# Turning y of later groups on VectorE instead of TensorE: a fused two-layer residual kernel in fp32r halves

## The reference, cut to what matters

```python
x = x + (einsum('bsd,bdh->bsh', x, L0_W[cat]) + L0_b[cat][:, None, :])        # y
h = gelu(einsum('bnd,hd->bnh', x, fc1_w) + fc1_b)                            # exact gelu
shared = einsum('bnh,sh->bns', h, fc2_w) + fc2_b                              # 384 columns
expert = einsum('bnh,bph->bnp', h, experts_w[idx]) + experts_b[idx][:, None, :]   # 128 columns
out = x + concatenate([shared, expert], -1)
```

## Time and profile before

| | |
|---|---|
| three runs, median | 1683.79 us |
| the profiled execution, own time | 1683.98 us |
| its span | 1682.1 us |
| mean granted clock of TensorE | 0.995 |
| TensorE busy | 1663.5 us (99%) |
| VectorE, ScalarE, Pool busy | 1146.4, 555.2, 200.4 us |
| read from and written to memory | 194.20 and 16.78 MB |

### The profile page before, as it was taken

The page is one execution under the profiler, slowest core; times in us unless marked ns, Lnnn a source line. Parts: engine busy times, 40 slices in busy tenths (PEclk is TensorE's granted clock), DMA queues, the critical chain, the costliest instruction groups (busy, mean ns, idle before and its releaser), DMA issues.

```text
span 1682.1 us, 27867 instructions
## 1 busy us (share of the span) xinstructions
PE 1663.5 (99%) x7305; PEld 1344.5 (80%) x7305; DVE 1146.4 (68%) x1944; ACT 555.2 (33%) x927; POOL 200.4 (12%) x195
## 2 busy tenths in 40 slices
PE   7899999999999999999999999999999999999999
PEld 4688888888888888888888888888888888888887
DVE  4677767677676766857767676776767667676654
ACT  4343233233333333333333333333333333332321
POOL 0010200101010110200202011110200102001010
PEclk8999999999999999999999999999999999999999
DMA  7875546555565565655555465555655546565430
GB/s 208 182 177 129 124 110 150 118 134 119 115 155 106 140 128 104 143 120 136 120 125 130 108 158 110 134 125 110 151 115 132 128 100 146 117 141 119 97 51 25
DMA packets 749465, 211.95 MB, mean 126 GB/s; under 512 B 676008, under 2 KB 690488, under 8 KB 749372
## 3 DMA queue, kind: packets, MB, share of 16 engines
q1 hardware_dynamic: 740732, 203.75, 55.2%
q10 hardware_dynamic: 8640, 7.34, 1.5%
HBM read 194.20 MB, written 16.78 MB: 125 GB/s over the span
## 4 chain that ended last, share of the span: by engine, by line
PE 97%; SPq 1%; DMA 1%; issue 0%; DVE 0%; ACT 0%; DVEq 0%
PE ps_out L732 43%; PE ps_e L717 21%; PE ps_h L717 21%; PE ps_y L704 10%; PE ps_t L654 1%; PE ps_e L654 1%; SPq L333 1%; SPq L313 0%; DMA prep_raw<-in_L_cond_fc_w 0%; SPq L286 0%; DMA w_raw<-in_L_cond_W 0%; DMA exps<-in_itok_B 0%; DVE resid L590 0%; PE ps_h L704 0%; PE ps_h L702 0%
## 5 line engine op out<-in xcount | busy, mean ns | idle before, releaser
L732 PE MATMUL ps_out<-w2e,h 128*128 128x512 f32 x3072 | 761.8, 396 | 0.0
L732 PEld LDWEIGHTS ps_out<-w2e,h 128*128 128x128 f32 x3072 | 573.6, 188 | 135.0
L717 PE MATMUL ps_h<-y_t,w 128*128 128x512 f32 x1536 | 376.9, 395 | 0.0
L717 PE MATMUL ps_e<-y_t,w 128*128 128x512 f32 x1536 | 375.5, 394 | 1.4 <-DVE y_t L520 1.4
L717 PEld LDWEIGHTS ps_e<-y_t,w 128*128 128x128 f32 x1536 | 290.0, 189 | 65.8 <-DVE y_t L520 1.8
L717 PEld LDWEIGHTS ps_h<-y_t,w 128*128 128x128 f32 x1536 | 288.7, 188 | 66.7
L442 ACT CAST w_split<-w_raw 128x512 fp32r<-128x512 f32 x256 | 157.8, 617 | 301.4 <-PE ps_y L704 284.3
L520 DVE TENSOR_TENSOR w_split<-w_raw,w_split 128x512 fp32r<-128x512 f32 x256 | 185.8, 726 | 95.2 <-ACT w_split L442 94.9
L578 DVE CAST h<-g_raw 128x512 fp32r<-128x512 f32 x256 | 116.4, 455 | 191.5 <-ACT g_raw L471 190.9
L409 POOL TENSOR_TENSOR x_raw<-x_raw,b_all 128x512 f32<-128x512 f32 x60 | 79.0, 1317 | 1338.5 <-DMA x_raw<-in_x 1338.5
L457 ACT CAST w2e<-e_whole 128x512 fp32r<-128x512 f32 x256 | 158.7, 620 | 190.8 <-PE ps_out L732 190.8
(11 more groups left out here) (56 smaller groups left out, 422.9 us busy)
## 6 DMA issues: line engine op xcount, KB each, us to landing
w_raw<-in_L_cond_W SPq DMA_DIRECT2D x256, 256.0 KB, 2.9
e_blocks<-in_L_cond_experts_w SPq DMA_DIRECT2D x1024, 64.0 KB, 2.5
out<-resid SPq DMA_DIRECT2D x64, 256.0 KB, 3.3
x_blocks<-in_x SPq DMA_DIRECT2D x240, 64.0 KB, 2.4
b_all<-in_L_cond_b SPq DMA_DIRECT2D x60, 256.0 KB, 3.4
x_raw<-in_x SPq DMA_DIRECT2D x60, 256.0 KB, 3.1
prep_raw<-in_L_cond_fc_w ACTq DMA_DIRECT2D x27, 256.0 KB, 3.9
be_all<-in_L_cond_experts_b SPq DMA_DIRECT2D x64, 64.0 KB, 3.0
```

Of the source, the lines that this page charges most:

```text
L717: last = nc.tensor.matmul(h_bank(c)[:, :], w1[:, w, k, c * P:(c + 1) * P], y_t[:, a, k, :, :].rearrange("p b s -> p (b s)"), start=(k == 0 ...
L732: last = nc.tensor.matmul(ps_out[b][:, :], h[:, c % 2, a, b * S:(b + 1) * S], fc2_columns(c, c % 2, w, b), start=(c == 0 and n == 0), stop ...
```

## The change

- The four turns of y of every later group leave TensorE. ScalarE's queue stores each y to an internal DRAM tensor y_rows (store_y, the step after y_sum) and, at the end of that step, loads it back as exchanged blocks into x_blocks (load_y_blocks, four transfers); VectorE transposes it two steps after y_sum (turn_y). The four turned batches are kept in two tiles of w_raw (y_hold), in x_whole_t and in ps_t until y_high and y_low at the end of the body, which now wait for the group's last fc1 themselves.
- L0's slices go in pairs in the steps of L0_STEPS, so that the last is done in step 12 and not 15.
- W of later groups has two places (WSLOTS = 2); in the first group eight, four of them in the half of e_blocks that is free then (W0SLOTS). b0_rows moves to y.
- SP's order: experts one step earlier (c % 4 of 0 and 1), store(g - 1) at step 2 after the loads of steps 0 and 1, load_x_blocks of batches 0 to 3 at steps 0, 1, 6 and 10; in the start, the experts begin at j = 8, two transfers a slice; the first loads of group 1 and the biases come in step 0 of body(0).
- Pool's add_out_bias waits for y_ready instead of y_turned.

```diff
-    WSLOTS = 4
+    WSLOTS = 2
+    W0SLOTS = 8
+    L0_STEPS = (1, 3, 5, 7, 9, 10, 11, 12)
...
-        w_raw = sb("w_raw", [P, WSLOTS, D])
+        w_raw = sb("w_raw", [P, WSLOTS + 2, D])
...
+        y_hold = w_raw[:, WSLOTS:WSLOTS + 2, :]
+        y_rows = nc.dram_tensor("y_rows", (GB, P, D), F32, kind="Internal").ap()
...
+            return four((y_hold[:, 0, :], y_hold[:, 1, :], x_whole_t[:, :], ps_t)[b])
...
+        def slices_in(c):
+            return [2 * p + i for p, step in enumerate(L0_STEPS) if step == c for i in range(2)]
+        def begun_in(c):
+            return [b for b in range(GB) if L0_STEPS[2 * b] == c]
+        def summed_in(c):
+            return [b for b in range(GB) if L0_STEPS[2 * b + 1] == c]
... SP
+                if b == 0:
+                    after(sp, y_turned, G * GB)
+                elif b == 1:
+                    after(sp, x_turned, G * GB + 1)
+                else:
+                    after(sp, y_turned, G * GB + b - 1)
...
+            def load_l0_in(G, c):
+                for b, step in ((0, 0), (1, 1), (2, L0_STEPS[1] + 3), (3, L0_STEPS[3] + 3)):
+                    if c == step:
+                        load_x_blocks(G, b)
+                for p in range(2 * GB):
+                    if c == (0 if p == 0 else L0_STEPS[p - 1]):
+                        if p % 2 == 0:
+                            load_l0_in.cat = category(G, p // 2)
+                        load_w(G, 2 * p, load_l0_in.cat)
+                        load_w(G, 2 * p + 1, load_l0_in.cat)
+                for b in range(GB):
+                    if c == (0 if b == 0 else L0_STEPS[2 * b - 1] + 1):
+                        load_b0(G, b, load_l0_in.cat)
+                        load_x(G, b)
...
+                    if c == 2 and not first(g):
+                        store(g - 1)
+                    if more:
+                        load_l0_in(g + 1, c)
-                    if c % QUAD in (1, 2):
+                    if c % QUAD in (0, 1):
... ScalarE
+                after(act, fc1_done, G * NC)
+                nc.scalar.copy(y_t[:, 0, :, b, :], y_whole(G, b)).then_inc(y_hi, 1)
+            def store_y(G, b):
+                after(act, y_ready, G * GB + b + 1)
+                act.dma_start(y_rows[b, :, :], y[:, b, :]).then_inc(y_stored, 16)
+            def load_y_blocks(G, b):
+                after(act, y_stored, 16 * ((G - 1) * GB + b + 1))
+                if b + 1 < GB:
+                    after(act, x_turned, G * GB + b + 2)
+                else:
+                    after(act, y_turned, G * GB + b)
+                for i in range(P // Q):
+                    src = y_rows[b, :, :].rearrange("(j q) (k i r) -> i q k j r", q=Q, k=KD, r=Q)[i]
+                    act.dma_start(x_blocks[i * Q:(i + 1) * Q, :].rearrange("q (k j r) -> q k j r", k=KD, r=Q), src)\
+                       .then_inc(y_blocks_in, 16)
...
+                        for j in slices_in(c):
+                            w_high(g + 1, j)
+                        for b in begun_in(c):
+                            x_high(g + 1, b)
+                        for b in summed_in(c - 1):
+                            store_y(g + 1, b)
                     e_high(g, c)
                     gelu(g, c)
                     for n in range(PREP_RATE):
                         prep_high(prep_in_step(g, c, n))
+                    if more:
+                        for b in summed_in(c - 1):
+                            load_y_blocks(g + 1, b)
... VectorE
+            def turn_y(G, b):
+                after(dve, y_blocks_in, 16 * (P // Q) * ((G - 1) * GB + b + 1))
+                dst = (y_hold[:, 0, :], y_hold[:, 1, :], x_whole_t[:, :], ps_t[:, :])[b]
+                nc.vector.transpose(dst, x_blocks[:, :]).then_inc(y_turned, 1)
... at the end of a step, after h_low and prep_low
+                        if c == 0:
+                            turn_x(g + 1, 0)
+                        for b in summed_in(c - 2):
+                            turn_y(g + 1, b)
+                        for b in summed_in(c):
+                            if b + 1 < GB:
+                                turn_x(g + 1, b + 1)
+                            y_sum(g + 1, b)
... TensorE
-                    if c == NC - 1:
-                        if more:
-                            l0_slice(g + 1, c - 1)
-                            l0_slice(g + 1, c)
-                            turn_y(g + 1, 0)
-                            turn_y(g + 1, 1)
+                    if c >= 1:
                         fc2(g, c - 1)
-                        if more:
-                            turn_y(g + 1, 2)
-                            turn_y(g + 1, 3)
-                    else:
...
+                    turn_prep(prep_in_step(g, c, 1))
+                    if more:
+                        for j in slices_in(c):
+                            l0_slice(g + 1, j)
                 fc2(g, NC - 1)
```

More of the change, by code:

```diff
@@ L110, in build @@
         prep_in = [sem(f"prep_in{i}") for i in range(PSLOTS)]
+        w0_in = [sem(f"w0_in{i}") for i in range(W0SLOTS)]
         w_in = [sem(f"w_in{i}") for i in range(WSLOTS)]
+        y_stored = sem("y_stored")
+        y_blocks_in = sem("y_blocks_in")
         x_blocks_in = sem("x_blocks_in")
@@ L303, in load_x_blocks, with load_w @@
                       .then_inc(x_blocks_in, 16)
[L305 to L309, removed]
-                        load_x_blocks(G, b)
[L312 to L322, removed]
+            def load_w(G, j, cat):
+                if first(G):
+                    after(sp, w_lo, j - W0SLOTS + 1)
+                else:
+                    after(sp, w_lo, G * NC + j - WSLOTS + 1)
+                k = j % KD
+                sp.dma_start(w_slot(G, j), l0_w[bass.ds(cat, 1), k * P:(k + 1) * P, :].rearrange("o d n -> (o d) n"))\
+                  .then_inc(w0_in[j % W0SLOTS] if first(G) else w_in[j % WSLOTS], 16)
@@ L353, in _ @@
             for j in range(NC):
-                load_l0(0, j // KD, j % KD)
+                if j % KD == 0:
+                    cat = category(0, j // KD)
+                load_w(0, j, cat)
+                if j % KD == 0:
+                    sp.dma_start(b0_rows[:, j // KD, :], l0_b[bass.ds(cat, 1), :]).then_inc(b0_rows_in[j // KD], 16)
                 if j % KD == KD - 2 and j // KD + 1 < GB:
                     load_first_x(j // KD + 1)
[L357 to L364, removed]
                 if j == 1:
@@ L529, in w_low @@
                 after(dve, w_hi, G * NC + j + 1)
[L530 removed]
+                minus(w_split[:, j % 2, 1, :], w_slot(G, j), w_split[:, j % 2, 0, :]).then_inc(w_lo, 1)
             def turn_x(G, b):
@@ L614, in body @@
                     if more:
-                        if c == 0:
-                            turn_x(g + 1, 0)
-                        w_low(g + 1, c)
-                        if c % KD == 0:
-                            x_low(g + 1, c // KD)
+                        for j in slices_in(c):
+                            w_low(g + 1, j)
+                        for b in begun_in(c):
+                            x_low(g + 1, b)
                     if c == 1 and not first(g):
@@ L634, in body @@
                     prep_low(prep_in_step(g, c, 0))
-                    if more and c % KD == KD - 1:
-                        y_sum(g + 1, c // KD)
                     h_low(g, c)
                     prep_low(prep_in_step(g, c, 1))
-                    if more and c % KD == KD - 2 and c + 2 < NC:
-                        turn_x(g + 1, c // KD + 1)
+                    if more:
[7 more added lines that the diff above has]
+                            y_sum(g + 1, b)
                 if more:
@@ L661, in turn_x, with turn_y @@
                 turn(ps_t, [resid[:, b, k * P:(k + 1) * P] for k in range(KD)]).then_inc(x_turned, 1)
-            def turn_y(G, b):
-                after(pe, y_ready, G * GB + b + 1)
-                if first(G):
-                    if b == 0:
-                        pe.wait_ge(b1_ready, 1)
-                    after(pe, y_lo, b)
-                elif b == 0:
-                    if first(G - 1):
-                        pe.wait_ge(prep_lo, NPREP)
-                elif b == 1:
-                    after(pe, gelu_done, G * NC - 1)
-                else:
-                    after(pe, y_lo, G * GB + b - 1)
-                turn(y_bank(G, b), [y[:, b, k * P:(k + 1) * P] for k in range(KD)])\
+            def turn_y(b):
+                pe.wait_ge(y_ready, b + 1)
+                if b == 0:
+                    pe.wait_ge(b1_ready, 1)
+                after(pe, y_lo, b)
+                turn(y_bank(b), [y[:, b, k * P:(k + 1) * P] for k in range(KD)])\
                     .then_inc(y_turned, 1)
```

74 lines of the change are left out of this document (40 added, 34 removed).

## The result

The changed kernel takes 1764.78 us (median of four runs, 1763.94 to 1768.69), the kernel before beside it 1683.91: a ratio of 1.048, 95% interval 1.0467 to 1.0494. I had forecast 1662.6 us, faster, with a range to 1681. The forecast is wrong, and in sign.

What follows compares the result with a forecast made beforehand. TensorE was taken to bound the kernel after the start, with no idle time to win. From 1683.98 us: -26.4 (turns), +4 (tight places), +4 (first group), -3 (start) gave 1662.6 us, range 1652 to 1681.

Steps and rivals of the forecast that it cites:

- What goes: Group ends: four turns of y leave TensorE, 1.76 us a group at 15 boundaries, 26.4 us saved.
- Step 5: Mid groups: w_low and x_low end at T(5)+4.9, needed at +5.6; tight places together 0.3 us a group.
- Step 11: Mid groups, tightest place: inputs ready at T(11)+5.5, needed at +5.6; tight places together 0.3 us a group.
- rival C: Two W slots: late slices stall TensorE some 2.6 us in step 11 of each group; 1697.6 us; chance 0.13.
- Rival B: Pool's adds stall step 5, and 9 or 11: 1 to 1.5 us a group, 1673 to 1680 us; chance 0.20.
- The traffic: DMA: 240 more block loads add about 9 points to the engines' share; room, but landings may lengthen.
- Group 0: First group: two waits of 2 us before weight turns, after y's block loads; +4 us, bounds 0 and 8.
- The start: Before fc1: eight W slots bring the weights sooner; -3 us, bounds -6 and +1.
- Boundary: Between groups: y_low(3) ends T(15)+7.2, needed at +8.4; fc1 waiting for y_lo priced at nothing.

Runs made afterwards that it cites:

- h5: h3 with four of eight expert loads moved one step later, behind the W of slices 12 and 13: 1662.42 us, ratio 0.987.
- g2: Changed kernel with all four results of g-1 added in step 0 on VectorE, none in step 1: 1767.30 us.
- e4: Changed kernel without y's store and the wait for it, the four block loads kept but reading x (bounds a time, not usable): 1689.81 us.
- h3: f2 with own buffers for y's blocks, x_blocks(2) and (3) before experts, last experts in steps 8 and 9, y's loads one step later: 1685.53 us, ratio 1.0013.
- e2: Changed kernel with y of later groups turned by TensorE again, without y's store, block loads and VectorE turn: 1714.74 us.
- e3: Changed kernel without y's store and block loads, VectorE still turning the buffer's old content (bounds a time, not usable): 1682.37 us.
- f2: Changed kernel, same work reordered: results in step 0, store(g-1) before experts, y_sum before turn_x, Pool's output adds in a row: 1683.53 us, ratio 1.000.

## Why the prediction was wrong

- **What goes, 26.4 us: right.** h5's period of 100.1 is 101.88 - 1.76. The Trainium skill's 275 ns for a transpose ("TensorE: Matmul & The Clock Gate", Part 4: PE-mode transpose) would have taken 4.4 us off a group (an estimate from that page's figure); the measured 0.11 us each decides.
- **Step 5, priced at 0.3 us a group with 0.7 us of slack: the failing step.** Its terms in the group shown: y_sum(0) ended at T(4)+3.9, not +1.6 (store issued at T+19.9 and not 17, resid ready at T+26.6, not 23); from there to the last of the four loads' issue it took 6.9 us, not 6.3 (the wait for the store was right within 0.2 us, the loads took 3.08 us, not 2.4); w_high and x_high 0.1 us more; the two w_low and x_low ended 1.9 us behind x_high, not 0.9 (two w_low 2.34 us beside Pool, 1.3 without). x_low ended at 639.4, T(5)+9.0, and not at +4.9: 4.1 us late, less the 0.7 of slack, 3.4 us of stall. More than half, 2.3 us, is the late store ahead of y_sum(0), and that term alone was over the slack; the rest are errors of 0.1 to 1.0 us, all one way and in series with it. The bounds I had set, 0 to 2 us a group, treated them as one small uncertainty.
- **The clock after a stall: left out.** I had named the lower clock for the start alone; 35.4 us of the result are slower matmuls, at a mean granted clock of 0.977 against 0.995.
- **Step 1: missed.** fc2(0) of batches 2 and 3 waits for result(g-1, 2 and 3), and the changed steps put two w_low and x_low before them. 0.90 us, free in the changed kernel (g2), 1.0 us a group once the rest is in order (e4).
- **Step 11: its slack of 0.1 us right, its price too low**, 0.2 to 1.2 us a group. The mechanism of rival C (W behind the experts, two slots) is real: in h3 it is the only stall, and h5 shows that moving four transfers ends it. But it was not what made the change slow; C had put its 2.6 us there, and they came in step 5.
- **Rival B** had the Pool part of step 5, some 1 us of the 4.1, and no more; its ceiling of 1.5 us a group was the same error.
- **The traffic** of 240 more block loads is 10.5 points by its own terms (55.2 x 240 / 1264), not 9; it moved nothing in the sum.
- **Group 0: +4 forecast, +13.1 measured** (11.3 longer and the 1.76 that went), with three stalls before weight turns. Two follow block loads of y, as forecast, in steps 5 and 9: 2.77 and 3.06 us, not 2. The third and largest, 3.85 us, I did not have, and it is not y's. It comes before the first store of y:

```profile
76.91 0.71 DVE L638 STREAM_TRANSPOSE e_whole<-e_blocks 128x512 f32<-128x512 f32 x1 [4.64 <-DMA e_blocks<-in_L_cond_experts_w]
...
78.63 0.63 PE L737 MATMUL ps_t<-ident,prep_raw 128*128 128x128 f32 x4 [3.85 <-issue]
...
82.35 0.38 ACTq L509 DMA_DIRECT2D y_rows<-y  x1
```

  VectorE waits for the experts' blocks in the changed order of SP, and the low half of the weight tile stands behind their turn. It is there without any transfer of y (4.55 us in e2, 3.06 in e3, with 4.18 and 4.03 us of the same wait) and nearly gone in h5 (0.73).
- **The start: -3 forecast, -0.2 measured** (fc1 at 45.52). With eight slots the start's last weight cast begins at 37.18 us, before the change at 37.94, so its data came hardly sooner.
- **Boundary: right.** fc1(0) never waited for y_lo in a mid group.

The forecast's number, 1662.6, is that of h5 by chance of terms: there the start is worth 0.1 us and the mid groups' stalls next to nothing, and group 0 costs 2.5 us net of its 1.76.

## What to carry to other kernels

In these runs a queue that waited for a transfer held everything behind it: put such a wait behind the work that the bounding engine needs next, not ahead of it, even if the data is then later. Where a saturated engine is to lose work, list for each of its waits the slack after the change, and add the errors of a chain's terms instead of pricing them as one; when a slack is under the sum of them, count on the stall, and on slower matmuls after it. Follow each list to its end before pricing it: the largest term here was a store that stood 20 us down SP's list. And when several stalls stand in a row, cutting the first may give nothing, and cutting the last link in front of the engine may give all.

## What the runs showed of the hardware

- A store of 256 KB followed by a wait on its landing took 2.2 to 2.7 us (f2, 13 of 14 groups) and 3.6 to 4.2 us (the changed kernel) from issue to the next issue, both at step 4; what made the difference was not tested.
- A tensor_tensor of VectorE that overlaps a Pool instruction can take twice its time: w_low at most 0.69 us alone and up to 1.80 beside Pool (the changed kernel).
- Four block loads with fixed addresses took 2.65 to 3.08 us on ScalarE's queue, against SP's 2.99 with register work.
- After 3.4 us of idle TensorE's granted clock was 0.50 for the next six matmuls and back at full within the twelve behind them (0.83 over the 10 us around it); after 0.9 us the rows show next to nothing (1.66 us for six instead of 1.54).
- The DMA share of a mid group rose from 0.56 or 0.58 before the change to 0.69 or 0.70 in h5, and TensorE never waited for it.
